# Weight sums of the Strassen groups on GpSimd in place of VectorE

## What is computed

```
gate = x Wg' + lora;  up = x Wu' + lora
c = (silu(gate) * up) Wd' + lora          # 1376 inner features
nx = c * rsqrt(mean(c^2) + eps) * ln_w
out = x + (silu(nx Wg2') * (nx Wu2')) Wd2'  # 1792 inner features
```

## Time and profile before

| | |
|---|---|
| median of 3 runs | 397.09 us (396.99 to 397.59) |
| profiled execution, first to last instruction | 395.5 us |
| TensorE busy | 391.8 us (99%) |
| VectorE busy | 314.8 us (80%) |
| ScalarE busy | 240.8 us (61%) |
| GpSimd busy | 10.6 us (3%) |
| granted TensorE clock, mean | 0.999 |

### The profile page before, as it was taken

One profiled execution on the slowest core, in us unless ns is written; L12 is line 12 of the kernel. 1 busy time (PEld: TensorE's weight loads), 2 busy tenths in 40 slices (PEclk: granted clock), 3 DMA queues, 4 the chain that ended last, 5 costly groups with the idle time before them and its releaser, 6 DMA issues.

```text
span 395.5 us, 5733 instructions
## 1 busy us (share of the span) xinstructions
PE 391.8 (99%) x1984; PEld 327.3 (83%) x1984; DVE 314.8 (80%) x476; ACT 240.8 (61%) x386; POOL 10.6 (3%) x13
## 2 busy tenths in 40 slices
PE   9999999999999999999999999999999999999997
PEld 5899888888888888888888888888888888888885
DVE  4899979586835869578699787878787869899994
ACT  5969786857574469815745656464646494484740
POOL 6300000000000000000000000000000000000000
PEclk9999999999999999999999999999999999999999
DMA  7640243311111551000400021313130316105112
GB/s 271 182 133 0 83 133 98 110 53 55 53 55 54 164 154 57 2 0 0 159 2 1 12 97 55 106 53 108 60 119 37 89 57 199 55 1 201 54 53 108
DMA packets 14942, 32.42 MB, mean 82 GB/s; under 512 B 2370, under 2 KB 4930, under 8 KB 14914
## 3 DMA queue, kind: packets, MB, share of 16 engines
q1 hardware_dynamic: 13792, 30.22, 23.7%
q10 hardware_dynamic: 1122, 1.84, 1.3%
HBM read 29.95 MB, written 2.10 MB: 81 GB/s over the span
## 4 chain that ended last, share of the span: by engine, by line
PE 99%; DVE 0%; issue 0%; DVEq 0%
PE bank L1365 53%; PE bank L1705 17%; PE bank L1593 14%; PE bank L1511 3%; PE bank L1557 3%; PE bank L1546 3%; PE bank L1375 3%; PE bank L1615 1%; PE bank L1607 1%; PE bank L1505 1%; PE bank L1714 0%; PE bank L1622 0%; DVE act L1354 0%; DVEq L1352 0%
## 5 line engine op out<-in xcount | busy, mean ns | idle before, releaser
L1365 PE MATMUL bank<-xs,ws 128*128 128x512 f32 x840 | 195.0, 390 | 0.0
L1365 PEld LDWEIGHTS bank<-xs,ws 128*128 128x128 f32 x840 | 156.6, 188 | 31.9
L415 ACT ACTIVATE xs<-act 128x512 fp32r<-128x512 f32 x71 | 42.8, 623 | 21.1 <-DVE act L1045 7.6
L1593 PE MATMUL bank<-xs,wdc 128*128 128x512 f32 x240 | 55.7, 390 | 0.0
L1593 PEld LDWEIGHTS bank<-xs,wdc 128*128 128x128 f32 x240 | 44.8, 188 | 9.5 <-issue 0.2
L889 DVE TENSOR_TENSOR xs<-act,xs 128x512 fp32r<-128x512 f32 x71 | 47.5, 685 | 2.7 <-ACT xs L415 2.1
L889 DVE TENSOR_TENSOR ws<-wraw,ws 128x256 fp32r<-128x256 f32 (+2 forms) x45 | 30.0, 668 | 13.0 <-ACT ws L415 12.8
L415 ACT ACTIVATE bank<-bank 128x512 f32<-128x512 f32 x30 | 17.3, 580 | 34.5 <-PE bank L1365 33.7
L415 ACT ACTIVATE mu<-bank 128x512 f32<-128x512 f32 x44 | 26.1, 596 | 20.1 <-PE bank L1365 13.6
L1705 PE MATMUL bank<-xs,vs 128*128 128x512 f32 x168 | 38.2, 389 | 0.0
L1705 PEld LDWEIGHTS bank<-xs,vs 128*128 128x128 f32 x168 | 31.5, 188 | 6.5
(11 more groups left out here) (133 smaller groups left out, 439.5 us busy)
## 6 DMA issues: line engine op xcount, KB each, us to landing
wraw<-wgu_in SPq DMA_DIRECT2D x22, 512.0 KB, 3.3
wdr<-vs_in SPq DMA_DIRECT2D x7, 512.0 KB, 3.6
wraw<-vj_in SPq DMA_DIRECT2D x3, 896.0 KB, 4.7
wdr<-wd_in SPq DMA_DIRECT2D x10, 256.0 KB, 2.7
xa<-xT_in SPq DMA_DIRECT2D x4, 256.0 KB, 4.1
xa<-xT_in ACTq DMA_DIRECT2D x2, 512.0 KB, 4.7
bgu_raw<-bgu_in SPq DMA_DIRECT2D x32, 32.0 KB, 1.9
xres<-xT_in SPq DMA_DIRECT2D x4, 256.0 KB, 3.5
```

The source lines that it names most:

```text
L415: return nc.scalar.activation(out_ap, in_ap, ACT.Copy, scale=scale)
L1365: ins = mm(z[:, :], w_slot(j)[:, w, s, k * P:(k + 1) * P], xs[:, c, r, k, :], start=(start and k == 0 and s == 0 and r == 0), stop=(k == 1 ...
L1593: ins = mm(z[:, :], wd[:, s, h * P:(h + 1) * P], x[r], start=(start and s == 0 and r == 0), stop=False, skip_group_check=True)
```

## The change

`sums(j)` goes from VectorE to GpSimd, for all 22 groups, with the same instructions, buffers and waits. GpSimd makes the groups in the order of j behind its paddings; the memset of `ad` stands between j = 9 and j = 10. `lo_b` on VectorE gets a wait for the third sum.

```diff
-            pool.wait_ge(s_stklo, 8)
-            nc.gpsimd.memset(ad[:, :, :, RANK:2 * RANK], 0.0).then_inc(s_ad_pad, 1)
+
+            def sums(j):
+                g = j - 2
+                pool.wait_ge(s_w_ld[j % 2], 16 * (j // 2))
+                if g >= 1:
+                    pool.wait_ge(s_wbhi, w_of(g - 1) - 1)
+                    pool.wait_ge(s_wblo, w_of(g - 1) - 1)
+                raw_w = wraw[:, j % 2, :, :]
+                nc.gpsimd.tensor_tensor(wsum[:, 0:2, :], raw_w[:, 1::2, :], raw_w[:, 0:1, :].to_broadcast([P, 2, 256]),
+                                        ALU.add).then_inc(s_wsum, 1)
+                pool.wait_ge(s_wsum, 3 * g + 1)
+                nc.gpsimd.tensor_tensor(wsum[:, 2, :], wsum[:, 1, :], raw_w[:, 1, :], ALU.add).then_inc(s_wsum, 1)
+                pool.wait_ge(s_wsum, 3 * g + 2)
+                nc.gpsimd.tensor_tensor(wsum[:, 3, :], wsum[:, 2, :], raw_w[:, 2, :], ALU.add).then_inc(s_wsum, 1)
+
+            pool.wait_ge(s_act_pad, 1)
+            pool.wait_ge(s_pad, 4)
+            for j in range(2, G2):
+                if j == G1:
+                    pool.wait_ge(s_ad_pad, 1)
+                sums(j)
+                if j == G1 - 1:
+                    pool.wait_ge(s_stklo, 8)
+                    pool.wait_ge(s_wsum, 3 * (j - 1))
+                    nc.gpsimd.memset(ad[:, :, :, RANK:2 * RANK], 0.0).then_inc(s_ad_pad, 1)
...
-            def sums(j):
...
             def lo_b(j):
                 v.wait_ge(s_wbhi, j - 1)
+                v.wait_ge(s_wsum, 3 * (j - 2) + 3)
                 part = w_slot(j - 2)
...
-            sums(2)
...
-                if w_next(j) < last:
-                    sums(w_of(w_next(j)))
...
-                    sums(G1 + (n - 5) // 2)
...
-            sums(G1 + 2)
...
-            sums(G1 + 3)
```

## The result

The changed kernel takes 400.15 us (median of 4 runs, 399.94 to 400.36); the kernel before took 397.04 us beside it (4 runs, 396.77 to 397.59). The ratio is 1.0076, with a 95% interval of 1.0064 to 1.0088: about 3.1 us slower. The profiled execution spans 398.6 us against 395.5, which is the same 3.1 us, so the trace can be read for all of it. The granted TensorE clock is 1.000 in it.

What follows compares the result with a forecast made beforehand. The prediction took TensorE's own work as the bound (busy 391.8 of 395.5 us). Stalls of 0.95, 2.2, 0 and 0.65 us sum to 3.8, added to 397.1 for 400.9 us; range 396.9 to 402.4.

Steps and rivals of the forecast that it cites:

- the relief at 0: Taking 33.7 us of weight sums off VectorE gains nothing, as TensorE waits for nothing that VectorE makes.
- The duration on GpSimd: One group of three sums takes 2.5 us on GpSimd, between bounds of 1.53 and 2.7.
- The collision: GpSimd and two-SBUF-input VectorE instructions take turns; each GpSimd instruction adds its whole duration to a VectorE chain.
- Steady groups: Ordinary groups of both stages: `c22_sum` delayed 0.1 to 0.6 us, TensorE needing it 1.27 us after its end; cost 0.
- Place A: Start of the kernel: early sums of j = 2 make `t_lo` 1.88 us late; TensorE stalls 0.95 us.
- cover: Time from the end of the producer's row until TensorE starts on what it made; delay beyond it becomes stall.
- Place B: Second norm: sums of j = 14 fall into VectorE's chain up to `lo_t(1, 0)`; TensorE stalls 2.2 us.
- Place C: wx groups: sums of j = 13 end 0.9 to 1.8 us later; 0 in the sum, 0.2 in the high case.
- Place E: First group behind the wx groups: sums of j = 15 delay `c22_sum` by 2.5 us; TensorE stalls 0.65 us.
- Nothing collides: Rival: the engines read side by side without delay, so the time stays 397.1 us; chance 0.15.
- One turn in a gapless run: Rival: GpSimd gets one instruction into a gapless VectorE run, then waits for a gap; 398.4 us, chance 0.12.
- Twice as slow: Rival: GpSimd takes 5 us a group, twice the assumed duration; near 411 us, chance 0.08.

Runs made afterwards that it cites:

- hold_three: Changed kernel with GpSimd's sums of j = 2, 14 and 15 each held back behind VectorE's work there: 397.27 us, ratio 1.0001.
- beside_add: Kernel before, sums still on VectorE, plus idle two-input GpSimd adds from j = 4 on that nothing waits for: 398.43 us, ratio 1.0032.
- beside_memset: Kernel before, sums still on VectorE, plus idle GpSimd memsets from j = 4 on that nothing waits for: 397.01 us, ratio 0.9996.
- hold_start: Changed kernel with GpSimd's sums of j = 2 held back until VectorE has made lo_t(0,1), behind t_lo: 398.92 us, ratio 1.0045.

## Why the prediction was right, and where its sizes were off

**What bounds the kernel, and the relief at 0.** Right. TensorE is still busy for 99% of the span, and `hold_three` is the measurement: 17 us less work for VectorE, ratio 1.0001. One number beside it was wrong: VectorE's busy time was to fall to 281 us and is 301.9. I had counted the delays only in the chains that TensorE waits for, and the steady groups collide too.

**The duration on GpSimd.** I took 2.5 us for a group between bounds of 1.53 and 2.7. Alone it takes 2.76, just above the upper bound, which was built from one write and two reads at the memset's rate. That was the nearest of the three estimates, and the estimate from the Trainium skill ("GPSIMD Engine Reference", section 3.1), 2.25, was farther off.

**The collision.** Right in kind: this was the step that no row of before could show, and `beside_add` against `beside_memset` shows it by itself. Wrong in size: "each instruction of GpSimd adds its whole duration to a chain of VectorE". The turns by whole instructions are there; the price is not the whole instruction. A 512-column add costs VectorE 0.9 to 1.1 us of its 1.29 (by the starts of the rows 0.91 at B, 1.10 at A), a 256-column one 0.4 to 0.6 of its 0.74. The same holds against the lock for a whole instruction that the prediction quotes from the Trainium skill ("SBUF — State Buffer", section "Who interferes with whom"): the trace agrees that one engine waits until the other's instruction is done, but what VectorE waits is shorter than GpSimd's row. So a group costs 1.5 us (two of three adds, at A) or 1.87 (all three, at B) rather than 2.5. My duration was too short and this share too large; at B the two errors do not cancel but leave 0.6 us too much.

**Steady groups at 0.** Right: TensorE's shift goes only from 1.05 at 28 to 1.12 at 193, and it is 2.89 at 232 and 3.1 at the end of the program, with the 0.2 of place E in between.

**Place A, 0.95.** Measured 0.84. The path was the one described, VectorE's last row late by 28.10 - 26.37 - 0.21 = 1.52 us and not 1.88. The stall is 0.84 and not 1.52 - 0.93 = 0.59 because TensorE started 0.25 us behind the end of `tgu` (28.35 against 28.10), a handoff that my cover had counted as free. The two errors offset.

**Place B, 2.2.** Measured 1.65 (1.72 with what follows). At `lo_t(1, 0)` the delay is 2.99 less the 1.17 us of shift that TensorE had by then, 1.82 us; less the cover of 0.27 it gives 1.55. That is the term, mis-sized by the share above. What I did not see is the first half of the stall. I followed VectorE's chain only, but ScalarE's queue has the copy of a bank, `save(S1 + 3)`, behind a conversion that waits for the scalings. TensorE shifted there by 2.09 - 1.17 = 0.92 already, and by 0.73 more at `g_prod(8)`. The sum is the same, since the later reader sets it; with a little more cover at `lo_t` the ScalarE path would have been the whole stall. In `hold_start` TensorE's only wait there is the one for `sqr`.

**Place C, 0.** Right: 0.05. **Place E, 0.65.** Measured 0.09, or 0.2 with the next product. `c22_sum` ends at 234.94, 4.76 later than before and 1.87 later than the shift of 2.89. Against a cover of 1.83 that is almost nothing. A term that is the difference of two numbers of 2 us takes over the whole error of one: 2.5 against 1.87.

**The sum.** 3.8 forecast and 2.9 measured at the places (with what follows them), 3.1 with the 0.2 us at the start that is no part of the change. The times, each with its own holds: without A 398.92, without B 398.65, without all three 397.27.

**The rivals.** *Nothing collides* falls with the VectorE rows at 24.10 and 26.45. *One turn in a gapless run* falls with place B, where all three adds ran inside the four scalings, none waiting for a gap. *Twice as slow* falls with 2.76 us for a group, although a group beside gapless two-input work comes near it: 1.30 + 2.09 + 2.13 = 5.5 us in `hold_start`. Even that would not have given its price, since there GpSimd waits for VectorE's instructions, and VectorE goes on meanwhile.

## What to carry to other kernels

Moving work from an engine that nobody waits for bought nothing here, and the idle engine was not free: GpSimd's two-input adds delayed VectorE's two-input instructions. Price such work by its effect on every chain of VectorE that it will now lie beside. Work that a full queue had put behind a critical chain starts as soon as its data lands on an idle engine. One added wait at each of the three places, on the end of the chain there, took the whole loss back. When taking a cover, follow each engine that waits for the late tile, what stands behind it in that engine's queue, and leave something for the handoff: 0.25 us lay between the end of `tgu` and its reader, 0.05 and 0.1 us at the two waits of place B.

## What the runs showed of the hardware

- A GpSimd add (two fp32 inputs from SBUF) and a VectorE instruction with two inputs from SBUF take turns by whole instructions. Beside gapless work of VectorE a 512-column add takes 1.6 to 2.2 us instead of 1.29 and a 256-column one up to 2.2 instead of 0.74, and it ends 1.15 or 0.6 us behind the VectorE row that it found running.
- VectorE loses less than the add's own duration: 0.9 to 1.1 us for 512 columns and 0.4 to 0.6 us for 256.
- GpSimd is not shut out by a run of VectorE without gaps. Its instructions got one turn in each of the first three of the four scalings.
- A VectorE row with one input in a bank kept its 0.68 us with a GpSimd add running beside it (288.97 beside 288.63 to 289.92).
- A one-input copy of GpSimd (721 ns on average for 512 columns) also delays two-input rows, by 0.08 to 0.29 us each at place B; a memset (530 ns) by nothing.
